# Value rows copied to channels in halves of a chunk, and one row tile for three scales

## The reference

```
x  = ln(x); xn = ln(x)                            # scales rs0, rs1
r, k, v, g, a, decay = projections of xn and of its shift by one step
kk = k * k_k / norm per head of (k * k_k)         # scale rk
for t in range(T):                                # 16 heads of 8 x 8 state
    sa    = sum_j state[i, j] * a_t[j]            # a_t = -kk
    state = state * d_t[j] + sa[i] * b_t[j] + v_t[i] * k_t[j]
    out_t[i] = sum_j state[i, j] * r_t[j]
out = groupnorm(out) + bonus; x = x + (out * g) @ W_o
x   = x + relu(ffn)^2; then router, four experts, layer norm
```

## Time and profile before

| | |
|---|---|
| median of 3 runs | 1195.27 us (1194.85 to 1198.77) |
| time of the profiled execution | 1195.53 us |
| its span, first to last instruction | 1193.7 us |
| TensorE matmul, busy | 1054.8 us, 88% |
| VectorE, busy | 940.2 us, 79% |
| GpSimd, busy | 650.4 us, 54% |
| ScalarE, busy | 605.3 us, 51% |
| DMA queue of SyncE | 136392 packets, 74.33 MB, 31.0% of 16 engines |
| value transfers | 512 of 64 KB |

### The profile page before, as it was taken

One profiled execution on the slowest core, in us unless ns is written; L12 is line 12 of the kernel. 1 busy time (PEld: TensorE's weight loads), 2 busy tenths in 40 slices (PEclk: granted clock), 3 DMA queues, 4 the chain that ended last, 5 costly groups with the idle time before them and its releaser, 6 DMA issues.

```text
span 1193.7 us, 19599 instructions
## 1 busy us (share of the span) xinstructions
PE 1054.8 (88%) x6099; PEld 713.3 (60%) x6099; DVE 940.2 (79%) x2283; ACT 605.3 (51%) x965; POOL 650.4 (54%) x885
## 2 busy tenths in 40 slices
PE   4676689999998999999998989999999999988976
PEld 2243356666565757666665757566666656666755
DVE  4468778898989888898988888898889888876320
ACT  2424364736465574637464564647364654733341
POOL 0246665665656656566656666665556566555200
PEclk9769899999999999999999999999999999999989
DMA  3324123342424233432424232333425233221110
GB/s 126 67 40 75 33 45 71 63 89 42 100 47 86 56 61 69 78 72 52 94 42 96 56 74 56 67 71 62 90 41 102 45 84 57 52 58 36 37 27 18
DMA packets 136496, 75.58 MB, mean 63 GB/s; under 512 B 15292, under 2 KB 129980, under 8 KB 136264
## 3 DMA queue, kind: packets, MB, share of 16 engines
q1 hardware_dynamic: 136392, 74.33, 31.0%
HBM read 11.35 MB, written 4.19 MB: 13 GB/s over the span
## 4 chain that ended last, share of the span: by engine, by line
PE 36%; DVE 20%; SPq 19%; issue 10%; ACT 8%; DMA 6%; POOL 0%; DVEq 0%; ACTq 0%; POOLq 0%
SPq L314 10%; SPq L301 6%; PE fin_b L564 6%; PE fin_a L564 5%; DMA val_rep<-val_c 5%; PE sa_ps L405 5%; DVE state L898 4%; PE mid_ps L356 4%; PE pre_a L356 3%; DVE upd L894 3%; PE var_ps L586 3%; ACT L600 3%; SPq L298 3%; DVE kv L871 2%; DVE s_a L884 1%
## 5 line engine op out<-in xcount | busy, mean ns | idle before, releaser
L1071 POOL TENSOR_TENSOR plus_kv<-state,kv 128x128 f32<-128x128 f32 x512 | 283.3, 553 | 406.1 <-DVE state L898 383.1
L405 PE MATMUL sa_ps<-s_a,con 128*128 128x128 f32 x1024 | 226.0, 303 | 55.8 <-DVE s_a L884 53.2
L405 PEld LDWEIGHTS sa_ps<-s_a,con 128*128 128x128 f32 x1024 | 172.3, 193 | 168.7 <-DVE s_a L884 137.7
L1063 POOL TENSOR_TENSOR s_r<-state,r_t 128x256 f32<-128x256 f32 x256 | 244.7, 956 | 3.3 <-DVE state L898 3.3
L894 DVE TENSOR_TENSOR upd<-sa_ps,b_t 128x128 f32<-128x128 f32 x512 | 146.2, 286 | 84.6 <-PE sa_ps L405 80.7
L898 DVE TENSOR_TENSOR state<-upd,plus_kv 128x128 f32<-128x128 f32 x512 | 191.8, 375 | 17.6
L884 DVE TENSOR_TENSOR s_a<-state,a_t 128x128 f32<-128x128 f32 x512 | 149.4, 292 | 18.5
L564 PE MATMUL fin_b<-h_e,mat 128*128 128x256 f32 x512 | 136.9, 394 | 4.0 <-ACT pick L770 4.0
L871 DVE TENSOR_TENSOR kv<-val_rep,k_t 128x512 f32<-128x512 f32 x128 | 117.8, 921 | 23.9 <-DMA val_rep<-val_c 23.3
L600 ACT ACT_TABLE_LOAD x101 | 129.6, 1283 | 1.8
L564 PE MATMUL fin_a<-h_e,mat 128*128 128x256 f32 x512 | 127.9, 379 | 0.0
(11 more groups left out here) (198 smaller groups left out, 1725.9 us busy)
## 6 DMA issues: line engine op xcount, KB each, us to landing
val_rep<-val_c SPq DMA_DIRECT2D x512, 64.0 KB, 2.4
rs_p<-row_rs SPq DMA_DIRECT2D x128, 64.0 KB, 2.1
x_in<-xT SPq DMA_DIRECT2D x16, 256.0 KB, 3.0
rs_p<-row_rk SPq DMA_DIRECT2D x64, 64.0 KB, 2.4
x_res<-xT SPq DMA_DIRECT2D x16, 256.0 KB, 3.0
rs_m<-row_frs SPq DMA_DIRECT2D x64, 64.0 KB, 2.1
rs_f<-row_ers SPq DMA_DIRECT2D x64, 64.0 KB, 2.1
rs_f<-row_lrs SPq DMA_DIRECT2D x64, 64.0 KB, 2.1
```

The costliest lines, as they stand in the source:

```text
L405: mm(sa_ps[:, 0:STATE], k("sum8"), s_a[:], start=True, stop=True).then_inc(s["sa"], 1)
L1063: tt(part, states, r.unsqueeze(2).broadcast_to([128, 2, N, B]), ALU.mult).then_inc(s["s_r"], 1)
L1071: tt(plus_kv[:, (t % 2) * STATE:(t % 2 + 1) * STATE], st(t), kv[:, at:at + STATE], ALU.add).then_inc(s["plus_kv"], 1)
```

## The change

`replicate` copies a half of a chunk, not a quarter: 8 transfers of 128 KB (16 partitions, 1024 bytes of each repeated eight times), twice in a chunk. val_rep0 holds quarters 0 and 1, val_rep1 quarters 2 and 3; each is twice as large. "rep" has two places, -18 and 4 in AT, -9 and 4 in AT_FIRST, -11 and 1 in AT_LAST, the ones that quarters 0 and 1 had; those of quarters 2 and 3 go. The halves wait for kv of the same half of the chunk before. rs0, rs1 and rk share one row tile, and `rsqrt_row` waits for the transfers of the scale before it in the order rs0, rs1, rk, rs0 of the next chunk.

```diff
-    ... "rep": (-18, 4, 7, 11), ...
+    ... "rep": (-18, 4), ...
...
-        val_rep = [sb(f"val_rep{n}", N * QCOLS) for n in range(2)]
+        val_rep = [sb(f"val_rep{n}", N * 2 * QCOLS) for n in range(2)]
...
-        row = {n: sb(f"row_{n}", QCOLS) for n in ("rs0", "rs1", "rk", "frs", "ers", "lrs")}
+        row = {n: sb(f"row_{n}", QCOLS) for n in ("rs0", "frs", "ers", "lrs")}
+        row["rs1"] = row["rk"] = row["rs0"]
...
-            def replicate(c, q):
-
-                slot = q % 2
-                free = c.count(2 * (q - 2) + 2, 2 * QUARTERS)
-                free = free if isinstance(free, int) else settled(sp, free)
-                now = settled(sp, c.count())
-                if not isinstance(free, int) or free > 0:
-                    sp.wait_ge(s["kv"], free)
-                sp.wait_ge(s["val_c"], now)
+            def replicate(c, part):
+
+                if c.has(1):
+                    sp.wait_ge(s["kv"], (c + -1).count(4 * part + 4, 2 * QUARTERS))
+                sp.wait_ge(s["val_c"], c.count())
                 for i in range(N):
-                    heads = val_c[i * H:(i + 1) * H, q * QCOLS:(q + 1) * QCOLS].unsqueeze(1).broadcast_to([H, N, QCOLS])
-                    sp.dma_start(val_rep[slot][:, i * QCOLS:(i + 1) * QCOLS], heads).then_inc(s[f"val_rep{slot}"], 16)
+                    heads = val_c[i * H:(i + 1) * H, part * 2 * QCOLS:(part + 1) * 2 * QCOLS].unsqueeze(1).broadcast_to([H, N, 2 * QCOLS])
+                    to = val_rep[part][:, i * 2 * QCOLS:(i + 1) * 2 * QCOLS]
+                    sp.dma_start(to, heads).then_inc(s[f"val_rep{part}"], 16)
...
             def rsqrt_row(c, var, eps, n_in, n_ln, name, scale=1.0):
 
-                if c.has(1):
-                    act.wait_ge(s[name], (c + -1).count(64, 64))
+                shared = {"rs0": ("rk", -1), "rs1": ("rs0", 0), "rk": ("rs1", 0)}
+                sent, back = shared[name] if name in shared else (name, -1)
+                if c.has(-back):
+                    act.wait_ge(s[sent], (c + back).count(64, 64))
...
-                        act.wait_ge(s["val_rep0"], (c + -1).count(32 * N, 32 * N))
-                        act.wait_ge(s["val_rep1"], (c + -1).count(32 * N, 32 * N))
+                        act.wait_ge(s["val_rep0"], (c + -1).count(16 * N, 16 * N))
+                        act.wait_ge(s["val_rep1"], (c + -1).count(16 * N, 16 * N))
...
-                    dve.wait_ge(s[f"val_rep{q % 2}"], c.count(16 * N * (q // 2 + 1), 32 * N))
+                    dve.wait_ge(s[f"val_rep{q // 2}"], c.count(16 * N, 16 * N))
...
-                values = val_rep[q % 2][:, half * 4 * QCOLS:(half + 1) * 4 * QCOLS]
-                tt(part, values.rearrange("p (i t b) -> p i t b", i=N // 2, t=QUARTER),
+                values = val_rep[q // 2][:].rearrange("p (i t b) -> p i t b", i=N, t=2 * QUARTER)
+                values = values[:, half * 4:half * 4 + 4, (q % 2) * QUARTER:(q % 2 + 1) * QUARTER]
+                tt(part, values,
```

More of the change, by code:

```diff
@@ L28 @@
     "c0": -32, "sq0": -31, "x_in": -31, "j0": -29, "rs0": -29, "x1": -27, "d_rs0": -24, "xh0": -24,
[2 rows of a table removed]
-    "mix_r": -15, "mix_v": -15, "w2": -14, "th_d": -13, "rk": -13, "mix_g": -13, "kks": -13, "val_c": -12,
-    "v": -11, "cum": -10, "p": -10, "k2": -9, "val": -9, "r": -8, "kk": -8, "val_sb": -8,
[2 rows of a table added]
+    "mix_v": -15, "w2": -14, "th_d": -13, "rk": -13, "mix_g": -13, "kks": -13, "val_c": -12, "v": -11,
+    "cum": -10, "p": -10, "k2": -9, "val": -9, "r": -8, "kk": -8, "val_sb": -8,
     "keep": (-7, 1, 1, 1, 14, 28, 62, 93, 94, 95, 95), "k_t": -7, "r_t": -7, "rec": -6, "a_t": -5, "rkb": -5,
@@ L50 @@
     "k": -15, "mix_r": -15, "w2": -14, "mix_g": -13, "kks": -13, "d_rk": -11, "v": -11, "val": -11, "k2": -11,
-    "val_c": -10, "cum": -10, "r": -10, "val_sb": -9, "rep": (-9, 4, 5, 11), "kk": -8, "r_t": -8, "a_t": -8,
-    "p": -7, "k_t": -7, "rkb": -6, "g1": -6, "rec": -6, "rkb_ps": -5, "kki": -5, "b_t": -4, "th_g": -3,
-    "g2": -2, "gate": -2, "bonus": -1, "bonus_b": 1, "x_res": 28, "gsq": 34, "grs": 35, "gj": 36, "gxh": 38,
[3 rows of a table removed]
-    "pick_sb": 61, "h": 63, "router": 63, "y1b": 63, "best": 64, "onehot": 64, "masks": 64,
-    "h_e": (65, 65, 67, 68), "pick": 65,
+    "val_c": -10, "cum": -10, "r": -10, "val_sb": -9, "rep": (-9, 4), "kk": -8, "r_t": -8, "a_t": -8, "p": -7,
+    "k_t": -7, "rkb": -6, "g1": -6, "rec": -6, "rkb_ps": -5, "kki": -5, "b_t": -4, "th_g": -3, "g2": -2,
+    "gate": -2, "bonus": -1, "bonus_b": 1, "x_res": 28, "gsq": 34, "grs": 35, "gj": 36, "gxh": 38, "fsq": 39,
+    "gaff": 39, "gg": 39, "wo": 40, "x2": 41, "fc": 41, "frs": 42, "d_frs": 42, "fj": 44, "x2x": 47, "xf": 47,
+    "fxh": 48, "hid": (51, 52, 57, 59), "kf": 52, "f1": (52, 52, 53, 54, 54, 55, 56, 56), "d_ers": 53,
+    "f2": (56, 57, 57, 58, 58, 58, 58, 58), "y1": 59, "ec": 59, "ej": 59, "esq": 60, "ers": 60, "pick_sb": 61,
+    "h": 63, "router": 63, "y1b": 63, "best": 64, "onehot": 64, "masks": 64, "h_e": (65, 65, 67, 68),
+    "pick": 65,
     "moe": (66, 66, 66, 67, 68, 69, 69, 69, 70, 70, 70, 70, 70, 71, 71, 71, 74, 75, 75, 75, 76, 76, 77, 77, 78, 79, 79, 80, 80, 80, 81, 81),
@@ L67 @@
     "wa": -16, "dx": -16, "th_d": -15, "mix_k": -15, "k": -15, "mix_r": -15, "mix_v": -15, "rk": -15,
-    "w2": -14, "val_c": -14, "mix_g": -13, "v": -13, "kks": -12, "p": -12, "cum": -11, "rep": (-11, 1, 3, 11),
+    "w2": -14, "val_c": -14, "mix_g": -13, "v": -13, "kks": -12, "p": -12, "cum": -11, "rep": (-11, 1),
     "k2": -9, "val": -9, "val_sb": -9, "r": -8, "kk": -8, "k_t": -7, "r_t": -7, "rec": -6, "a_t": -5,
@@ L301, in over_channels @@
                         sp.dma_start(to[:, g * QCOLS:(g + 1) * QCOLS], rows).then_inc(s[name], 16)
-            def replicate(c, q):
-                slot = q % 2
-                free = c.count(2 * (q - 2) + 2, 2 * QUARTERS)
-                free = free if isinstance(free, int) else settled(sp, free)
-                now = settled(sp, c.count())
-                if not isinstance(free, int) or free > 0:
-                    sp.wait_ge(s["kv"], free)
-                sp.wait_ge(s["val_c"], now)
+            def replicate(c, part):
+                if c.has(1):
+                    sp.wait_ge(s["kv"], (c + -1).count(4 * part + 4, 2 * QUARTERS))
+                sp.wait_ge(s["val_c"], c.count())
                 for i in range(N):
-                    heads = val_c[i * H:(i + 1) * H, q * QCOLS:(q + 1) * QCOLS].unsqueeze(1).broadcast_to([H, N, QCOLS])
-                    sp.dma_start(val_rep[slot][:, i * QCOLS:(i + 1) * QCOLS], heads).then_inc(s[f"val_rep{slot}"], 16)
+                    heads = val_c[i * H:(i + 1) * H, part * 2 * QCOLS:(part + 1) * 2 * QCOLS].unsqueeze(1).broadcast_to([H, N, 2 * QCOLS])
+                    to = val_rep[part][:, i * 2 * QCOLS:(i + 1) * 2 * QCOLS]
+                    sp.dma_start(to, heads).then_inc(s[f"val_rep{part}"], 16)
             def work(c, at):
-                for q in range(QUARTERS):
-                    if at == c.place["rep"][q]:
-                        replicate(c, q)
+                for part in range(2):
+                    if at == c.place["rep"][part]:
+                        replicate(c, part)
                 if at == c.place["d_rs0"]:
```

## The result

The changed kernel takes 1210.82 us (median of 4 runs, 1209.98 to 1211.78), the kernel before 1195.06 us beside it (4 runs, 1194.19 to 1198.77): a ratio of 1.0132, with a 95% interval of 1.0112 to 1.0152. The forecast was 1214, in a range of 1193 to 1236. The profiled execution has a span of 1209.8 us against 1193.7, so there are 16.1 us to account for.

The account below looks back on a forecast made before the run. SyncE's issue of value transfers was taken to bound two places per chunk, with VectorE and TensorE nearly full between. Sum: 1195.5 - 4 (last quarter) + 20.7 (slower landing) + 2.5 (start) = 1214.7; forecast 1214, range 1193 to 1236.

Parts of the forecast that it names:

- The last quarter: kv's 0.71 us wait for the last quarter's values goes; L683 starts 0.28 us earlier in 14 chunks: 4 us gained.
- the second quarter: Its values land with the first quarter's; kv's one wait of 0.95 us goes: up to 1 us gained, once.
- The source: Before the first quarter's kv, reading 16 partitions limits eight doubled transfers to 150 GB/s: landing 1.8 us later.
- Rival 1: Source doesn't limit; DMA engines keep up with 203 GB/s, landing moves 0.2 us: 1193 us; chance 0.19.
- Rival 3: 16 partitions are a hard limit, 101 GB/s, 5.2 us more per batch: 1271 us; chance 0.10 together with rival 4.
- the 1.8 to 2.5 given as a sign: Changed profile should show one wait a chunk, at the first quarter, of 1.8 to 2.5 us.
- Rival 4: Rows of 1 KB are cut in two, no issue saved, each longer: slower than rival 3; chance 0.10 together.
- 20.7 us: Loss from later landing at the first quarter: 9 chunks at 1.1 us plus 6 at 1.8 us.
- I take the issue as unchanged.: SyncE issues the larger transfers before the first quarter no slower, as a 2 KB-row transfer took 0.59 us.
- I take it as passed on whole.: The later kv at the first quarter delays the scan and next chunk's row_rk by its full length.
- The start: First chunk's 16 doubled value transfers delay the second chunk's x_in by 3.5 us, of which 2.5 counted.
- The covers: Shared row tile's waits, row_lrs transfers queued behind the larger batch and val_c overwriting add nothing; a lost cover costs tenths of a microsecond a chunk.

Follow-up runs that it names:

- this part alone: Kernel before with quarters 2 and 3 in 128 KB transfers, in first chunks behind x_in; quarters 0 and 1 as before; shared row tile: 1191.46 us, ratio 0.9967.

## Why the prediction was right, and where it was wrong

*The last quarter: right.* No wait is left there, L683 gained 0.34 us against 0.28 forecast, and the kernel with this part alone gained 3.9 us against 4 (and up to 1 for the second quarter), with 1.4 us at the end, which the forecast had at nothing, taken off. The reading that carried it was what would be late next: of 0.7 us of idle time only 0.3 led on.

*The source: right in cause, as far as it was tested.* Reading 128 partitions once takes the whole loss away; whether it is the number of partitions or the repeated reading that costs isn't shown. Rival 1 fell with the landing of 3.2 us, where it needed 2.6. Rival 3 fell too: the last landing moved by 1.0 us and not by 5.2, and the values flowed at 150 GB/s in the window, where 101 was its limit. The waits at the first quarter are 1.8 us on the mean, the low end of the 1.8 to 2.5 given as a sign, and 1.3 to 2.2 in chunks 3 to 14. The Trainium skill's figure for 16 neighbouring partitions ("SBUF — State Buffer", section "Door 1: The DMA port swizzle"), 109 GB/s, which the page gives as the limit that large transfers come near, is for one such range. The eight transfers read eight ranges and together went above it; for a single one the extra 65.5 KB cost 0.8 us of landing (3.2 against 2.4), which is 82 GB/s and below it. The page says that partitions 64 apart reach other ports; no gain of that kind showed when such transfers followed each other.

*Rival 4* fell too: the queue has 99,528 packets, where the page of before shows 136,392. The difference of 36,864 is the 32,768 rows saved and 16 for each of the 256 transfers saved, so no row was cut.

*Its size: near, but made up otherwise.* The sum had 20.7 us for 15 chunks, 1.38 each, all of it flow. Measured are 1.0 us at the landing and 0.2 at the issue, 1.2 in all. Two steps of the argument were wrong in it:

- "I take the issue as unchanged." One value issue has a median of 674 ns, not 599, and in chunks 3 to 13 eight take 5.58 to 6.48 us where it was 5.04 to 6.25. The rows of 2 KB on which I based this were a single transfer. It is not the size that slows the issue: the same 128 KB read from 128 partitions go out with a median of 601 ns. In the view of the tile val_rep (duration of an issue in ns, min/median/max), first the changed kernel, then the one from 128 partitions:

```profile
L312 SPq DMA_DIRECT2D val_rep<-val_c x256: 544/674/1600, 42.7 to 1064.0; - x128
```

```profile
L312 SPq DMA_DIRECT2D val_rep<-val_c x256: 470/601/2153, 43.4 to 1042.6; - x128
```

  The issue takes longer in the kernel whose transfers land later; that the queue holds only so much is the likely reason, but only argued. The step of 0.645 us itself was divided wrongly: 568.54 is the start of the eighth issue, seven steps behind 563.37, so that batch has 0.74 each. 0.645 is right for the batches that are not held up, and the sum does not change.
- "I take it as passed on whole." Of the 1.2 us at kv, 0.34 are made up by the gain ahead of it, and of the 0.69 by which the medians leave kv later 0.2 are taken back before the next chunk (12.99 to 12.81). What takes them back I did not find. So a chunk loses 0.46 to 0.56 us, and 14 of them 6.4 to 7.8, where the sum had 20.7 - 4 = 16.7.

*The start: oversized.* 2.5 us forecast, 1.1 measured, and that is not clear of what two executions differ by. x_in went out at 54.76, after 16 issues that took 12.01 us and not 10.47, so the bytes delay it by 1.3, not the 3.5 that 150 GB/s would give.

*Not in the sum: the clock.* The wait leaves TensorE idle for some 1.5 us, and in three chunks the granted clock then falls to 0.50. That is 6.8 us, about what the steady chunks lose.

*Not in the sum: the end.* It takes 2.1 us more. It takes 1.4 more, with a short stretch at 0.50, also in both kernels with only the second half large (146.88 and 146.85 us), and no more in the one with only the first half large (145.31). So most of it goes with the second half's transfers and not with the longer wait; how is not shown.

These two filled what the two oversized terms had left: 1.1 + 6.4 + 6.8 + 2.1 = 16.4 against the 19.2 forecast. The right time came in part from errors that cancelled.

*The covers held.* y, which takes the row_lrs transfers, starts 2.93 us after kv (581.31 - 578.38), not later than the 3.15 of before (574.16 - 571.01). The shared tile costs nothing that can be measured.

*What stays open.* The parts don't add up in one place. The large first half costs 1.3 us a chunk on top of the kernel before (67.62 against 66.32, mean periods of the chunks at full clock), but 0.9 on top of the kernel with only the second half large (66.78 against 65.84). The landing moves by 1.0 us in both; the difference is in the issue of row_rk and the eight, which takes between 7.64 and 8.28 us in these kernels without a pattern that I could tie to an edit. Nor is it shown why the clock falls behind some of the long idle times only, nor by what path a transfer that reads 16 partitions eight times is slower than one that reads 128 once.

## What to carry to other kernels

Larger transfers save issue time only where the issue is what is late; where the last landing is what an engine waits for, more bytes in that batch are paid for at the landing. So merge the copies that have slack, here the second half (1191.46 us), and keep the one that is needed at once small. When copying within SBUF, look at how few partitions the source spans, and how often each is read, before its bytes. And where a wait grows, look at what TensorE does during it: filler work there, if it costs nothing, can keep the clock up.

## What the runs showed of the hardware

- A 128 KB transfer within SBUF that writes 128 partitions landed after 3.2 us when it read 16 partitions eight times, 2.7 from 32 four times and 2.2 from 128 once (median from issue). For 64 KB it was 2.4 from 16 and 2.1 from 32. With the same packets and bytes the queue's share of the DMA engines' time was 27.5, 25.6 and 22.5%.
- The issue of such a transfer took SyncE 674 ns (median) when it read 16 partitions and 601 ns when it read 128.
- Eight such transfers, each from another 16 partitions, flowed at 150 GB/s together in the window shown (packets of 1 KB alone), though the time that the second 64 KB add to a single landing would allow only 82.
- An idle time of 1.5 us on TensorE can cost 2.3 us more afterwards: the granted clock was 0.50 for 6.8 us in three chunks of the changed kernel, in four where only the first half was large (at 379.9, 516.5, 721.3 and 857.8), and in none of the steady chunks of the kernels with only the second half large, where TensorE idled 0.74 us at most at this place. All 13 such stretches between 250 and 1050 us in the traces of this case stand behind an idle time of 1.23 to 1.96 us. With fillers in it that idle time was 0.2 us or less, and there was no stretch; the median fell by 4.3 us.
